# Fourteen matmuls with an unread result in TensorE's two waits ahead of the first convolution

## What is computed

```python
# layer 0: a 64x64 mixing matrix of each batch row, made from cond by a small MLP; then fp8 product
y0  = einsum('boi,bih->boh', agg_w, x) + agg_b[:, :, None]
q   = (y0 / x_inv_scale).astype(float8_e4m3fn)          # one scale over the whole tensor
x1  = x + (q @ fp8_wt) * (x_inv_scale * w_inv_scale) + bias
# layer 1: grouped convolution along L (9 taps, 4 groups), then a product with dequantised 4-bit weights
y1  = conv_general_dilated(x1, weight, padding=4, feature_group_count=4) + ctx[:, :, None] + fside[None, :, None]
out = x1 + y1 @ W.T + bias1
```

## Time and profile before

| what | value |
|---|---|
| median of 3 runs | 532.83 us (531.87 to 533.1) |
| the profiled execution | 533.22 us, span 531.3 us |
| PE busy | 509.3 us, 96% |
| DVE busy | 410.6 us, 77% |
| ACT busy | 245.5 us, 46% |
| POOL busy | 60.4 us, 11% |
| mean granted TensorE clock | 0.994 |
| share of PE on the chain that ended last | 82% |

### The profile page before, as it was taken

The page is one execution under the profiler, slowest core; times in us unless marked ns, Lnnn a source line. Parts: engine busy times, 40 slices in busy tenths (PEclk is TensorE's granted clock), DMA queues, the critical chain, the costliest instruction groups (busy, mean ns, idle before and its releaser), DMA issues.

```text
span 531.3 us, 9515 instructions
## 1 busy us (share of the span) xinstructions
PE 509.3 (96%) x3495; PEld 286.1 (54%) x3526; DVE 410.6 (77%) x519; ACT 245.5 (46%) x287; POOL 60.4 (11%) x67
## 2 busy tenths in 40 slices
PE   4999999879999999999999999999999999999997
PEld 3644444345555555555555555555555555555563
DVE  4789999885887777777777777777777777777652
ACT  3488897655344444444444444444444444442310
POOL 6257775011000000000000000000000000000000
PEclk9999999979999999999999999999999999999999
DMA  6999491144665566666666656566565656566632
GB/s 185 399 394 400 159 350 66 47 114 101 202 199 179 179 180 182 181 183 185 185 186 185 183 179 179 179 179 179 179 179 179 179 179 182 179 187 186 200 121 79
DMA packets 85387, 100.22 MB, mean 189 GB/s; under 512 B 34348, under 2 KB 66862, under 8 KB 85374
## 3 DMA queue, kind: packets, MB, share of 16 engines
q1 hardware_dynamic: 84554, 99.29, 59.4%
q0 software_dynamic: 448, 0.55, 0.6%
q10 hardware_dynamic: 372, 0.20, 0.1%
HBM read 58.41 MB, written 32.75 MB: 172 GB/s over the span
## 4 chain that ended last, share of the span: by engine, by line
PE 82%; DVE 11%; issue 2%; POOL 2%; ACT 1%; DMA 1%; SPq 0%; POOLq 0%; DVEq 0%; ACTq 0%
PE pair L1156 42%; PE pair L1130 19%; PE pair L1146 17%; DVE stat L802 5%; PE pair L1038 2%; PE pair L1120 1%; DVE work L729 1%; PE pair L1026 1%; DVE work L817 1%; DMA work<-work 1%; POOL work L454 1%; DVE Y L817 1%; DVE work L732 1%; POOL fixed L487 1%; POOL Y L467 1%
## 5 line engine op out<-in xcount | busy, mean ns | idle before, releaser
L1156 PE MATMUL pair<-f1T,work 128*128 128x512 f16 x1024 | 231.0, 379 | 0.0
L1156 PEld LDWEIGHTS pair<-f1T,work 128*128 128x128 f16 x1024 | 98.9, 98 | 113.5
L608 ACT ACTIVATE work<-Y,consts 128x1024 bf16 (+1 forms) x29 | 33.3, 1148 | 186.7 <-DVE work L891 186.7
L910 DVE TENSOR_TENSOR work<-Y,work 128x512 f16<-128x512 f16 (+1 forms) x64 | 71.2, 1118 | 46.6 <-ACT work L641 45.6
L1130 PE MATMUL pair<-f0T,work 128*128 128x512 bf16 x435 | 98.6, 379 | 1.5
L1146 PEld LDWEIGHTS pair<-taps,work 128*128 128x128 f16 x1536 | 90.7, 99 | 9.8 <-issue 2.4
L1146 PE MATMUL pair<-taps,work 128*128 128x128 f16 x1536 | 93.4, 222 | 2.3 <-DMA work<-work 2.3
L923 DVE TENSOR_TENSOR Y<-pair,Y 128x512 f32 (+1 forms) x64 | 43.9, 687 | 44.2 <-PE pair L1156 44.2
L641 ACT CAST work<-Y 128x512 f16 (+1 forms) x64 | 69.5, 1135 | 17.9 <-DVE Y L900 15.6
L1130 PEld LDWEIGHTS pair<-f0T,work 128*128 128x128 bf16 x464 | 45.4, 98 | 54.8
L1038 PE MATMUL pair<-Y,work 128*128 128x512 f32 x128 | 61.8, 618 | 1.1 <-ACT Y L581 0.7
(11 more groups left out here) (150 smaller groups left out, 234.8 us busy)
## 6 DMA issues: line engine op xcount, KB each, us to landing
Y<-in_x_dram SPq DMA_DIRECT2D x64, 512.0 KB, 3.9
out_dram<-Y SPq DMA_DIRECT2D x31, 512.0 KB, 3.8
split_rows<-work SPq DMA_DIRECT2D x30, 520.0 KB, 2.6
work<-split_rows SPq DMA_DIRECT2D x30, 520.0 KB, 3.9
Y<-in_L_ffn_weight_dram SPq DMA_DIRECT2D x8, 512.0 KB, 6.5
Y<-in_L_ffn_W_q_dram SPq DMA_DIRECT2D x5, 512.0 KB, 14.6
work<-in_L_ffn_W_q_dram SPq DMA_DIRECT2D x3, 512.0 KB, 15.2
work<-work SPq DMA_DIRECT2D x8, 65.0 KB, 3.6
```

What stands on the lines that cost most here:

```text
L910: nc.vector.tensor_tensor(split[:, r, s, 1], v[:, r, :], split[:, r, s, 0], ALU.subtract)\
L1156: last = mm(ps[2 + h][:, :], y1s[n][:, e, k, :], f1T[:, k, h * H:(h + 1) * H], start=False, stop=(e == 1 and k == KT - 1), skip_group_chec ...
```

## The change

A helper, keep_clock(n), issues n matmuls of ident_b with 512 columns of f0T into ps[5]. Each opens and closes its own accumulation, and nothing reads the result. Four are issued behind the transposes of turned_first_q(2, 0), ten behind those of turned_first_q(2, 1). They wait for no semaphore and signal none.

```diff
@@ -1107,6 +1107,11 @@
                     last = nc.tensor.transpose(pb[:, k * P:(k + 1) * P], qn[t % 2][:, at:at + P], ident_b)
                 last.then_inc(q_turned, 1)
 
+            def keep_clock(n):
+
+                for _ in range(n):
+                    mm(ps[5][:, :], ident_b, f0T[:, 0, 0:H], start=True, stop=True)
+
             def first_ffn0(t, n, before):
                 for kh in range(2):
                     pe.wait_ge(qT_in[n], before + 8 * kh + 8)
@@ -1203,7 +1208,9 @@
             pe.wait_ge(x_step, 4)
             wsum_part(1)
             turned_first_q(2, 0)
+            keep_clock(4)
             turned_first_q(2, 1)
+            keep_clock(10)
             pe.wait_ge(taps_split, 4)
             conv(0, True)
             first_ffn0(2, 0, 16)
```

## The result

Median 531.58 us over 18 executions (530.47 to 534.03) against 533.46 for the kernel before over its 18 (531.87 to 535.33). The ratio is 0.9965 with a 95% interval of 0.9954 to 0.9976, that is 1.9 us faster, between 1.3 and 2.5. The profiled execution took 530.61 us, span 528.7, where the one of before had 533.22 and 531.3.

What follows compares the result with a forecast made beforehand. TensorE, busy for 96% of the span, was taken as the bound. Profiled 533.22 less 2.43 (convolution at full clock) plus 0.04 (copy wait) gave 530.83, 530.44 against the median, said as 530.5, range 529.5 to 531.9.

Steps and rivals of the forecast that it cites:

- the forecast: Whole kernel: clock stays up and the convolution's gain reaches the end; 530.5 us, own range 529.8 to 531.1; chance 76%.
- rivals 3: Second convolution, row copies of tile 1: they land late and it waits; between 530.9 and 532, say 531.5; chance 4%.
- Rival 4: Whole kernel: the median execution loses less than the profiled one; gain against the median 1.5 to 2.0, time 531.0; chance 8%.
- 5: Loop of 28 tiles: code sits 28 instructions further on, one more stop of 0.05 us per tile, 1.4; 531.8; chance 2%.
- Clock and convolution, -2.43: First convolution at 115.20 us: granted clock stays at 1.00, so it takes 2.84 us in place of 5.27, 2.43 less.
- two waits together: TensorE before the fall at 113.50: idle 1.00 us, 0.40 us of work, idle again; a single wait elsewhere brought no fall.
- Fillers, 0: Behind the (2, 0) and (2, 1) transposes: four hidden with 0.13 us to spare, ten with 0.12; cost 0, at most 0.2.
- What is late next: After the first convolution: its second half and ylo(0) cost 0, residual0(2) moves earlier, the second convolution waits 0.04 us.
- The wait for the row copies of tile 1, +0.04: Second convolution: wanted at 124.79, copies allow 124.83 at most, so a wait of 0.04 us; 0.2 kept for the range.
- The sum: Profiled execution: 533.22 - 2.43 + 0.04 = 530.83 us; against the median of three runs, 530.44.
- 1: Ramp: the clock falls anyway at 113.5 and the convolution makes up what slow fillers cost; no change, 532.8; chance 6%.
- 2: Ramp: same fall, clock's return counted from the convolution's start at 116.45; slower by 1.25, 534.1; chance 4%.

Runs made afterwards that it cites:

- experiment 2: The changed kernel's fourteen fillers cut from 512 to 32 columns; ratio 1.0007 against the kernel before, median 534.17 us beside 533.62.
- experiment 3: The changed kernel with only the four fillers, in the wait of 1.00 us, the ten removed; ratio 0.9951 against the kernel before, seven executions.
- 4: The changed kernel with only the ten fillers, in the wait of 2.29 us, the four removed; ratio 0.9962 against the kernel before, nine executions.
- experiment 6: The changed kernel's fourteen fillers at 256 columns in place of 512; median 532.25 us, ratio 0.9968 against the kernel before.
- experiment 1: The changed kernel run again with no edit; median 531.31 us over 10 executions, ratio 0.9962 against the kernel before.
- Experiment 5: The changed kernel with twenty fillers in place of ten in the wait of 2.29 us; median 532.6 us, ratio 0.9984 against the kernel before.
- experiments 7: The changed kernel plus six fillers further up, in TensorE's waits at 94.1 and 99.3 us; median 532.39 us, ratio 0.9983 against the kernel before.
- experiment 12: The changed kernel plus six early fillers and 32 matmuls of 32 columns in TensorE's wait at 52.2 us; median 530.82 us, ratio 0.9956 against the kernel before.
- experiment 8: The kernel before plus only six early fillers at 94.1 and 99.3 us, without the change's fourteen; median 534.4 us, ratio 1.0012 against the kernel before.
- 9: The changed kernel plus six early fillers narrowed to 32 columns; median 532.37 us, ratio 0.9981 against the kernel before.

## Why the prediction was right

It said 530.5 in 529.5 to 531.9, and 86% for faster by over 0.2%. Measured are 531.58 and 0.35%. The clock, the convolution and the way to the end were right. The time lies in the range given, but outside the forecast's own 529.8 to 531.1; it is inside only by the room left for rivals 3 to 5, none of which came as told. That much is luck.

*Clock and convolution, -2.43.* The profiled convolution is 2.43 shorter, to the digit, and its clock is 1.00 in all windows. That work causes it, and not the instructions, is shown by experiment 2, and from the other side by 3, 4 and 6. The idea from which I read the fall, two waits together, is borne out by 3 and 4: one wait filled was enough in 15 of their 16 executions, by the mean clock.

*Fillers, 0.* The four cost nothing. The ten were hidden too: in the profiled execution the convolution started 0.15 us after the fillers would have let it, close to the 0.12 that I counted on. My count began them at 112.92, when the transposes had ended; they began at 112.71, and the convolution itself started 0.14 earlier than in the trace before (with the 0.04 taken off by which that stretch lay earlier). In experiment 1's trace 0.40 us were left. Experiment 5 shows that what goes beyond the cover is paid in full.

*What is late next.* Second half of the convolution, ylo(0), residual0(2): all as worked out, the last with 0.25 us of VectorE's idle time left where I had 0.24. The wait for the row copies of tile 1, +0.04, is not there.

*The sum* was 530.83 for the profiled execution and is 530.61: 0.04 less for the wait that did not come, and 0.18 for the earlier start.

*The step that was off* is the one from that sum to the median: "against the median it is 530.44". The measured median is 1.1 us higher, and two things make it up. The median of three from which I started, 532.83, was low by 0.6: over 18 executions it is 533.46. And the gain by the medians is 1.9 where the prediction had 2.4. Executions of both kernels differ by a second fall of the clock, at 101 to 105 in the two traces that have it; by the mean clock it is in 11 of 28 executions of the changed kernel, which are about 1.7 us longer. The trace before was of an execution without it, so I had no row of it. The change does nothing about it; of the 18 executions of experiments 7 and 12, with the early stretch filled and the fourteen fillers in, none was at 0.997.

Like with like, the gain is what the sum said: 533.36 (median of the kernel before at 0.993 or 0.994) against 530.85 (of the changed kernel at 1.000) for executions without the early fall, and 534.90 (0.989 or 0.990) against 532.50 (0.996 or 0.997) for those with it, 2.5 and 2.4. The medians give less because the changed kernel's falls at the upper edge of its short group, and because the kernel before also has executions at 0.997, 16 of 86, with less to gain. These lie at 532.7. They may have a shorter fall in the ramp, as the two of experiment 8 seem to, or the early fall and none in the ramp, as their time is close to the 532.5 of the changed kernel with that fall. None of them has a trace, so that stays open.

Rival 4 had the gain by the medians, 1.5 to 2.0, but not the reason: it took the profiled execution to lose more than the median one, and over 18 executions the kernel before has its median above it, 533.46 against 533.22.

*Executions that differ.* The mean clocks of one program, the changed kernel, are 1.000 in 17 executions and 0.996 or 0.997 in 11. By the sentence of the Trainium skill that I had weighed (TensorE: Matmul & The Clock Gate, "It's run-variable"), the runs agree that one kernel's executions differ; the page speaks of the start of a kernel, and the falls here are at 101 and 113 us.

*The other rivals.* 1 and 2: no clock below 1.00 among the fillers in any trace that had them at work. Both counted the return of the clock, 5.1 us, from the start of unbroken work; experiments 2 and 8, with 5.7 and 3.9, show that this count does not hold, so their prices had no firm ground. 3: the row copies were in time. 5: no stop was added in the loop. The 0.05 us of idle time in each tile, from which I priced it, was none: the trace before lacks the records of 31 matmuls, the one of the changed kernel lacks none, and there TensorE is busy throughout:

```profile
122.00:250.00 128.00, 128.00 (x950) 1.00 0.63 183
```

The code's position did matter all the same, in a place where I hadn't looked (experiments 7 and 9).

## What to carry to other kernels

Where the granted clock drops behind a TensorE wait, look for what the low clock costs after the wait and fill the wait with matmuls that nothing reads; they are free up to the wait's length and cost their full time beyond it, so fewer are safer. Here four in the first wait did as much as fourteen in both, in seven executions; of nine with the ten alone, one was at 0.993. Look at the mean clock of many executions before trusting one trace: a fall can come in some of them only, at another place. And when instructions are added, compare where the instruction queue's packets lie, since one of them inside a load that is waited for can eat the gain.

## What the runs showed of the hardware

- The clock fell in the midst of unbroken TensorE work: in experiment 3's trace to 0.50 at 101.4, 1.5 us after TensorE's last wait (0.44 us, ending at 99.88), behind a stretch of light matmuls from 93. It stayed for 3.4 us, there and in experiment 6's trace. With only the first of the two waits of that stretch filled, by 0.87 us of fp32 or 0.43 us of bf16 work, 5 and 7 of 12 executions were at 0.997; with both filled, 0 of 12, and 0 of 6 in experiment 12. Whether the second wait alone would do was not tried.
- The fall in the ramp lasted 6.8 us in each of the three traces that have it (before, experiments 2 and 8), while the convolution began 1.7, 1.1 and 2.9 us after the fall and took 5.27, 5.28 and 4.68 us.
- With one 16 KB instruction packet in the middle of a 512 KB load, that load took 5.4 us in place of 3.6 at most. The packet does not move in step with the added instructions: twelve more put it at 103.6 or at 102.8 in place of 108.0, four more left it at 108.0 to 108.4, and with 76 more the one in this stretch was at 93.2 to 93.4. What decides when it is fetched stays open.
